# The last expert of a mixture layer worked in two halves, and ScalarE's read of a flag held behind seven experts' scatters

## The chip, the cores and the metric

The kernel runs on one core of a Trainium2 chip. The metric is the device time of one execution in microseconds (us), here the median of three runs. TensorE (PE) multiplies, VectorE (DVE) and ScalarE (ACT) do elementwise work, GpSimd (POOL) also issues the indirect DMAs, SyncE (SP) issues the plain ones.

## What is computed

Two layers of attention and feed-forward on x, 4 x 512 rows of 128 numbers. The change touches only the last piece, the second layer's mixture of experts with "expert choice": each of 8 experts takes the 256 rows that it scores highest, works them, and adds its result to those rows of the output.

```
route_prob = softmax(xf @ Ws + bs).T                 # [8, 2048]
route_vals, routes = top_k(route_prob, k)            # k = 256 rows for each expert
xin = xf[routes]
h = gelu(einsum('ekd,edf->ekf', xin, W1) + b1[:, None, :])      # 128 -> 512
out = (einsum('ekf,efd->ekd', h, W2) + b2[:, None, :]) * route_vals[..., None]
final = zeros.at[routes.reshape(-1)].add(out.reshape(-1, D))
```

## The kernel before

The program is written engine by engine; each engine runs its own list in order and waits on semaphores. About 150 us go to the two attentions, the first feed-forward layer and the search for each expert's rows. Then comes the stage of the change, `experts(again)`, written once for each engine, with `again` 0 here.

**Groups.** `GROUPS` lists pieces of work as (expert, first half, end half), where a half is 128 of an expert's 256 rows (`SH` is 2). Expert 0 is two groups of one half, experts 1 to 7 one group of two halves each, so `NG` is 9. Here k is a group's place in the list.

**One group.** GpSimd gathers each half's rows from DRAM (`gather`, L1936), which raises `got[e]`; expert 0's first half has a semaphore of its own, `got_first`. TensorE turns the rows (`rows_T`, L1337); ScalarE copies them out of PSUM (L858); TensorE makes the four chunks of the hidden layer (L1351); ScalarE puts bias and gelu on each (L863); TensorE makes y (L1363); VectorE adds a bias (L1736) and multiplies by the routing weight (L1738), which raises `y_done`. Then GpSimd adds each half's 128 rows to the output by an indirect DMA (`scatter`, L1944), which raises `out_add` by 16 when it has landed. Each of the 16 steps comes from one of the 16 DMA engines.

**What sets the order.** On GpSimd the list is: scatter both halves of expert e, gather the second half of e + 2, gather the first half of e + 3. So the first half of expert 7 is gathered ahead of expert 5's scatters, and its second half behind them. A scatter waits twice: for its group's `y_done`, and for the landing of all scatters of earlier experts, since two additions to one row must not cross:

```
pool.wait_ge(y_done, again * NG + (h + 1 if e == 0 else e + 2))
if n >= 1:
    pool.wait_ge(out_add, 16 * SH * n)
```

TensorE puts ten multiplications of no use (L911) between one group's y and the next group's turning, which keep its clock up. It turns group k + 1 right behind group k.

**The end.** Each engine, when through with its groups, reads a flag from memory and branches: if it is set, the whole work is done again by a slow general path, whose code stands between this point and the end of the engine's list; it isn't set here. ScalarE does so at L877 and L878, TensorE at L1375, VectorE at L1782. GpSimd reads the flag ahead of expert 6's scatters and branches at L1970 behind the last scatter. SyncE waits for all 16 scatters to land (`out_add` at 256). All engines then meet, which shows as line L102.

Of the kernel before, what the change touches and what calls it, by code (L numbers as in the profile page):

```python
# [33 lines left out]
E, F = 8, 512  # L34
FC = F // P
CAP = B * T // E
SH = CAP // P
# [6 lines left out]
BITS = 30  # L44
HEAD_GROUPS = ((0, 6), (6, 6), (12, 4))
FAST, SLOTS = 2, CH
GROUPS = ((0, 0, 1), (0, 1, 2)) + tuple((e, 0, SH) for e in range(1, E))
NG = len(GROUPS)
WARM = 10
INDEX_GROUPS = ((0, 1), (1, 4), (4, 8))  # L50
# [4 lines left out]

def chunk_rows(c):
    return min(CW, GK - c * CW)


def index_group(e):  # L60
    return [g for g, (e0, e1) in enumerate(INDEX_GROUPS) if e0 <= e < e1][0]
# [36 lines left out]
def program(nc, a, out):  # L98
# [3 lines left out]
    with ExitStack() as ctx:  # L102
# [3 lines left out]
        def sem(name):  # L106
            return ctx.enter_context(nc.semaphore(name))
# [131 lines left out]
        def logits(ps):  # L239
# [21 lines left out]
        ld_w = [sem(f"ld_w{e}") for e in range(E)]  # L261
        out_base, out_add = sem("out_base"), sem("out_add")
        rows_out = [sem(f"rows_out{b}") for b in range(B)]
        got_first, got = sem("got_first"), [sem(f"got{e}") for e in range(E)]
        consts_set, ctxT_ps_done, ctxT_done = sem("consts_set"), sem("ctxT_ps_done"), sem("ctxT_done")
        w_4_done = sem("w_4_done")
        k4_ps_done, k_hi_done, k_lo_done, k_stack_done, k_max_done = (
# [27 lines left out]
        xinT_ps_done, xinT_done, h_ps_done, gelu_done, y_ps_done, y_done = (  # L295
            sem(n) for n in ("xinT_ps_done", "xinT_done", "h_ps_done", "gelu_done", "y_ps_done", "y_done"))
# [53 lines left out]
        for n in range(E + 1):  # L350
# [5 lines left out]
            ("store", 32))  # L356
        LOADS = 32
        NAN_N, TILE_N = sum(n for _, n in NAN), sum(n for _, n in TILE)
        AFTER_NAN = LOADS + NT * NAN_N
        FLAGGED = 5  # L360
        TURNS_ALL = AFTER_NAN + FLAGGED + NT * TILE_N

        class Turns:


            def __init__(self, eng, stages, name, at):
                self.eng, self.at, self.k = eng, at + sum(n for _, n in stages[:[m for m, _ in stages].index(name)]), 0
# [113 lines left out]
        def run_tile(eng, i):  # L481
# [77 lines left out]
            if eng is nc.tensor:  # L559
# [7 lines left out]
                for g in range(G):  # L567
                    for c in range(GC):
                        n, o = chunk_rows(c), c * D + g * GD
                        go(); go.end(eng.matmul(bank[0][:, g * GD:(g + 1) * GD], wT[0:n, c, g, :], spans["v8"][0:n, o:o + GD],  # L570
                                                start=(c == 0), stop=(c == GC - 1)))
# [119 lines left out]
        def _(act):  # L691
# [72 lines left out]
            for ph in range(B):  # L764
                b = ph
                for s in range(SLOTS):
# [7 lines left out]
                    if b < B - 1:  # L774
                        n = chunk_rows(s // G)
                        nc.scalar.activation(pT[0:n, b % 2, s, :], ST_ps[s % 2][0:n, :], ACT.Exp).then_inc(exp_done, 1)  # L776
                    else:
                        half, i0 = 2 * s // SLOTS, s * PIECES % CH
                        n = chunk_rows(i0 // G)
                        nc.scalar.activation(pT[0:n, b % 2, i0:i0 + PIECES, half * HT:(half + 1) * HT],  # L780
                                             ST_ps[s % 2][0:n, :].rearrange("p (i t) -> p i t", i=PIECES), ACT.Exp).then_inc(exp_done, 1)
# [71 lines left out]
            def experts(again):  # L853

                for k, (e, h0, h1) in enumerate(GROUPS):
                    n, rows = again * NG + k, slice(h0 * P, h1 * P)
                    act.wait_ge(xinT_ps_done, n + 1)
                    nc.scalar.copy(xinT[:, k % 2, rows], bank[k % 2][:, rows]).then_inc(xinT_done, 1)  # L858
                    if n >= 2:
                        act.wait_ge(y_ps_done, n - 1)  # L860
                    for c in range(FC):
                        act.wait_ge(h_ps_done, n * FC + c + 1)
                        nc.scalar.activation(hg[:, k % 2, c, rows], bank[2 + c][:, rows], ACT.Gelu_apprx_tanh,  # L863
                                             bias=b1[:, e * FC + c:e * FC + c + 1]).then_inc(gelu_done, 1)

            def indices(again):

                act.wait_ge(own_base_done, again + 1)
                for e in range(E):
                    ins = nc.scalar.activation(cumx[:, e, :], pre[:], ACT.Identity, bias=own_base[:, e:e + 1], scale=own[:, e:e + 1])  # L870
                    if e + 1 in [e1 for _, e1 in INDEX_GROUPS]:
                        ins.then_inc(cumx_done, 1)

            act.wait_ge(once_done, 3)
            indices(0)
            experts(0)
            act.wait_ge(flag_done, 1)  # L877
            with act.If(act.value_load(flag[0:1, 0:1], min_val=0, max_val=1) > 0):  # L878
                with act.Fori(0, NT) as i:
# [7 lines left out]
        def _(pe):  # L887
# [438 lines left out]
            def rows_T(again, k):  # L1326
                n, (e, h0, h1) = again * NG + k, GROUPS[k]
                if h1 == 1:
                    pe.wait_ge(got_first, 16 * (again + 1))
                else:  # L1330
                    pe.wait_ge(got[e], 16 * (again + 1) * (h1 - h0))
                if k >= 2:
                    pe.wait_ge(xinT_done, n - 1)
                else:
                    pe.wait_ge(idx_done, again * len(INDEX_GROUPS) + k + 1)
                for h in range(h0, h1):
                    ins = pe.transpose(bank[k % 2][:, h * P:(h + 1) * P], xin[:, e, h, 0:D], ident)  # L1337
                ins.then_inc(xinT_ps_done, 1)

            def experts(again):  # L1340
                rows_T(again, 0)
                for k, (e, h0, h1) in enumerate(GROUPS):
                    n, rows = again * NG + k, slice(h0 * P, h1 * P)
# [52 lines left out]
        def _(dve):  # L1396
# [159 lines left out]
            with nc.allow_low_precision("a shift of the exponent that numerator and denominator share"):  # L1556
# [174 lines left out]
                def experts(again):  # L1731

                    for k, (e, h0, h1) in enumerate(GROUPS):
                        hs, shape = slice(h0, h1), [P, h1 - h0, D]
# [88 lines left out]
        def _(pool):  # L1823
# [71 lines left out]
            for ph in range(B):  # L1895
# [14 lines left out]
                if ph == 2:  # L1910
                    rows(0, 0)
            (ua, a0, a1, _, _), (ub, b0, b1_, _, _) = units(B - 1)
            t = B - 2
            ln_rstd(1, B - 1, ua, a0, a1)
# [14 lines left out]
            last_row = pool.to_reg(B * T - 1)  # L1929

            def gather(again, e, h):
                if (e, h) == (0, 0):
                    pool.wait_ge(idx_first, again + 1)
                else:
                    pool.wait_ge(idx_done, again * len(INDEX_GROUPS) + index_group(e) + 1)
                nc.gpsimd.indirect_dma_start(xin[:, e, h, :], None, gather_rows, bass.IndirectOffsetOnAxis(idx[:, h, e:e + 1], 0),  # L1936
                                             bounds_check=last_row, oob_is_err=False).then_inc(got_first if (e, h) == (0, 0) else got[e], 16)

            def scatter(again, e, h):
                n = again * E + e  # L1940
                pool.wait_ge(y_done, again * NG + (h + 1 if e == 0 else e + 2))
                if n >= 1:
                    pool.wait_ge(out_add, 16 * SH * n)
                nc.gpsimd.indirect_dma_start(flat, bass.IndirectOffsetOnAxis(idx[:, h, e:e + 1], 0), y[:, e, h, :], None,  # L1944
                                             bounds_check=last_row, oob_is_err=True, compute_op=ALU.add).then_inc(out_add, 16)

            def experts(again, first, last):

                for e in range(first, last):
                    if e == 0:  # L1950
                        for ahead in range(2):
                            for h in range(SH):
                                gather(again, ahead, h)
                        gather(again, 2, 0)
                    for h in range(SH):
                        scatter(again, e, h)
                    if e + 2 < E:
                        gather(again, e + 2, 1)
                    if e + 3 < E:
                        gather(again, e + 3, 0)  # L1960
# [38 lines left out]
```

## Time and profile before

| what | value |
|---|---|
| median of 3 runs | 217.88 us (217.6 to 218.38) |
| the profiled execution | 216.2 us, of which the span of the profile is 214.4 us |
| mean granted TensorE clock | 0.988 |
| busy in the span | PE 182.4, DVE 130.8, POOL 101.9, ACT 88.2 us |
| scatters (L1944) | 16, together 25.5 us of GpSimd |
| gathers (L1936) | 16, together 17.8 us of GpSimd |
| DMA queue q8, instructions | 12 packets, 0.20 MB |
| DMA queue q14, instructions | 12 packets, 0.10 MB |

The span runs from the first to the last instruction; 1.8 us of the profiled execution lie around it. A scatter's or gather's time on GpSimd is that of writing its descriptors; the data moves later, on queue q0. Queues q8 and q14 carry the program's own instructions to the engines, in one packet each time.

### The profile page before, as it was taken

To read this page: it belongs to the slowest core of one execution; us is meant where nothing else is said; L and a number is where in the kernel's file an instruction comes from. 1 tells how busy PE (TensorE), PEld (TensorE's weight loads), DVE (VectorE), ACT (ScalarE), POOL (GpSimd) and SP (SyncE) were. 2 spreads that over 40 slices of the span, in tenths; PEclk is the share of its full clock that TensorE was granted. 3 is DMA by queue.
4 is the path that set the end of the run, shared out by engine and by line. 5 is a ranking of instruction groups with operands and counts; after the bars stand their busy time and mean duration, and the time that the engine had idled before them with its cause. 6 is when DMAs were issued, how large, how long until landed. Compare 5 with 4: busy or idle time off the path is not lost.

```text
span 214.4 us, 3571 instructions
## 1 busy us (share of the span) xinstructions
PE 182.4 (85%) x1231; PEld 109.8 (51%) x1236; DVE 130.8 (61%) x450; ACT 88.2 (41%) x206; POOL 101.9 (48%) x111
## 2 busy tenths in 40 slices
PE   7988997979999978999999997998789877897730
PEld 2643543335334545376765764332277666786630
DVE  5887699077865889586789788887918111110110
ACT  2432772242622574246544452466443331333210
POOL 0699628000253022811048498200576788788722
PEclk9999999999999999999999999999999999999995
DMA  6634212111000001089810202100113232332313
GB/s 186 187 94 137 73 44 54 34 31 46 24 0 3 0 0 49 5 249 330 269 44 0 100 5 101 52 0 0 29 42 37 27 48 39 41 37 38 37 23 29
DMA packets 16127, 13.64 MB, mean 64 GB/s; under 512 B 3699, under 2 KB 13079, under 8 KB 16103
## 3 DMA queue, kind: packets, MB, share of 16 engines
q1 hardware_dynamic: 12246, 10.61, 16.6%
q0 software_dynamic: 2944, 2.30, 8.2%
q10 hardware_dynamic: 913, 0.43, 0.8%
q8 instruction: 12, 0.20, 0.4%
q14 instruction: 12, 0.10, 0.1%
HBM read 8.02 MB, written 3.21 MB: 52 GB/s over the span
## 4 chain that ended last, share of the span: by engine, by line
PE 41%; DVE 23%; POOL 14%; issue 10%; DMA 5%; ACT 3%; POOLq 1%; DVEq 0%
POOL out L1944 8%; PE psum L1009 7%; DVE mrow L1525 5%; DMA out<-pT,idx 4%; DVE pT L1671 3%; PE psum L906 3%; POOL pT L1936 3%; PE psum L1027 3%; DVE stats L1407 3%; PE psum L916 3%; DVE le L1721 2%; PE psum L979 2%; PE psum L1090 2%; PE psum L950 2%; PE psum L1046 2%
## 5 line engine op out<-in xcount | busy, mean ns | idle before, releaser
L1834 POOL TENSOR_SCALAR ve<-mv 128x4 f32<-128x4 f32 (+1 forms) x19 | 4.4, 232 | 69.4 <-DVE mv L1410 69.3
L776 ACT ACTIVATE pT<-psum 103x512 f32<-103x512 f32 (+1 forms) x36 | 21.2, 596 | 30.2 <-PE psum L981 30.2
L1944 POOL DMA_INDIRECT out<-pT,idx x16 | 25.5, 1594 | 11.2 <-issue 4.2
L1936 POOL DMA_INDIRECT pT<-gather_rows,idx x16 | 17.8, 1112 | 21.1 <-DVE idx L1725 17.1
L1525 DVE TENSOR_REDUCE mrow<-psum 128x8 bf16<-128x616 f32 x32 | 24.6, 788 | 5.1 <-PE psum L950 5.1
L906 PE MATMUL psum<-c 128*128 128x512 bf16 x103 | 26.5, 379 | 1.2 <-ACT key_map L801 1.0
L1736 DVE TENSOR_TENSOR pT<-psum,b_rows 128x256 f32<-128x256 f32 (+1 forms) x9 | 3.5, 394 | 36.2 <-PE psum L1363 36.2
L1351 PE MATMUL psum<-xinT,w 128*128 128x256 f32 (+1 forms) x72 | 16.2, 368 | 4.4 <-ACT xinT L858 3.2
L1552 DVE RECIPROCAL rden<-psum 128x512 f32<-128x512 f32 (+1 forms) x5 | 13.6, 2716 | 6.7 <-PE psum L1009 6.0
L1363 PE MATMUL psum<-w,pT 128*128 128x128 f32 x128 | 17.4, 284 | 0.2 <-DVE flag L1744 0.2
L863 ACT ACTIVATE pT<-psum,b 128x256 f32<-128x256 f32 (+1 forms) x36 | 14.4, 450 | 7.7 <-PE psum L1351 7.6
L1363 PEld LDWEIGHTS psum<-w,pT 128*128 128x128 f32 x128 | 16.2, 191 | 1.4 <-DVE flag L1744 0.3
L1351 PEld LDWEIGHTS psum<-xinT,w 128*128 128x128 f32 x72 | 12.0, 190 | 7.6 <-ACT xinT L858 5.9
L701 ACT COPY xnT<-psum 128x512 f32<-128x512 f32 (+1 forms) x19 | 9.8, 515 | 13.4 <-PE psum L916 13.3
L979 PE MATMUL psum<-q_stack,k_stack 128*103 128x512 f16 (+1 forms) x36 | 14.4, 401 | 0.8 <-DVE mT L1530 0.6
L906 PEld LDWEIGHTS psum<-c 128*128 128x128 bf16 x108 | 9.9, 99 | 9.6 <-ACT key_map L801 1.5
L858 ACT COPY xinT<-psum 128x256 f32<-128x256 f32 (+1 forms) x9 | 3.1, 349 | 26.7 <-PE psum L1337 26.7
L1838 POOL TENSOR_TENSOR rstd<-ve,half_neg 128x4 f32<-128x4 f32 (+1 forms) x14 | 13.4, 955 | 1.2
L981 PE MATMUL psum<-mT,neg_head 128*103 128x512 bf16 (+1 forms) x36 | 13.6, 379 | 0.0
L950 PE MATMUL psum<-k_max,q_hi 32*128 32x308 f16 x64 | 9.4, 299 | 4.3 <-DVE mrow L1525 3.9
L1846 POOL TENSOR_SCALAR xrow<-res,mv,rstd 128x128 f32<-128x128 f32 x16 | 12.6, 798 | 0.1
L950 PEld LDWEIGHTS psum<-k_max,q_hi 32*128 32x128 f16 x64 | 2.9, 91 | 16.2 <-DVE mrow L1525 10.7
(198 smaller groups left out, 370.3 us busy)
## 6 DMA issues: line engine op xcount, KB each, us to landing
w<-in_L_ffn_W SPq DMA_DIRECT2D x16, 256.0 KB, 5.5
gather_rows<-xrow SPq DMA_DIRECT2D x4, 272.0 KB, 2.1
x<-in_x SPq DMA_DIRECT2D x4, 256.0 KB, 4.1
q_stack<-q_hi SPq DMA_DIRECT2D x32, 32.0 KB, 1.8
out<-res SPq DMA_DIRECT2D x4, 256.0 KB, 2.1
q_stack<-q_lo SPq DMA_DIRECT2D x24, 32.0 KB, 1.9
b_rows<-in_L_ffn_b SPq DMA_DIRECT2D x1, 512.0 KB, 3.9
pT<-gather_rows,idx POOLq DMA_INDIRECT x16
```

The source lines that it names most:

```text
L776: nc.scalar.activation(pT[0:n, b % 2, s, :], ST_ps[s % 2][0:n, :], ACT.Exp).then_inc(exp_done, 1)
L863: nc.scalar.activation(hg[:, k % 2, c, rows], bank[2 + c][:, rows], ACT.Gelu_apprx_tanh, bias=b1[:, e * FC + c:e * FC + c + 1]).then_inc(g ...
L906: pe.matmul(bank[b][:, :], ident16, c16[:, 0:4 * P], start=True, stop=True)
L950: pe.matmul(bank[to + k][:, 0:GK], q_hi[rows, b % 2, j * P:(j + 1) * P], k_max[rows, b].rearrange("p h k -> p (h k)"), start=True, stop=Tr ...
L979: pe.matmul(ST_ps[s % 2][0:n, :], k_stack[:, b, g].rearrange("p h k -> p (h k)")[:, o:o + n], q_stack[:, b, g, :], start=True, stop=False)
L981: pe.matmul(ST_ps[s % 2][0:n, :], neg_head[:, g * GK + o:g * GK + o + n], mT[:, b % 2, :], start=False, stop=True).then_inc(st_ps_done, 1)
L1009: ins = pe.matmul(to[g * GD:(g + 1) * GD, :], lhsT, pT[0:n, b % 2, c * G + g, :], start=(c == 0), stop=(c == GC - 1), tile_position=(0, g ...
L1351: pe.matmul(bank[2 + c][:, rows], w1[:, e, c * P:(c + 1) * P], xinT[:, k % 2, rows], start=True, stop=True).then_inc(h_ps_done, 1)
L1363: ins = pe.matmul(bank[6 + k % 2][:, h * P:(h + 1) * P], hg[:, k % 2, c, h * P:(h + 1) * P], w2[:, e, c, :], start=(c == 0), stop=(c == FC ...
L1525: dve.tensor_reduce(mrow[:, b % 2, u // 2, h0:h0 + 2 * GH].rearrange("p (c h) -> p c h", c=2), psum[:, to:to + 2, 0:GK].rearrange("p c (h ...
L1936: nc.gpsimd.indirect_dma_start(xin[:, e, h, :], None, gather_rows, bass.IndirectOffsetOnAxis(idx[:, h, e:e + 1], 0), bounds_check=last_row ...
L1944: nc.gpsimd.indirect_dma_start(flat, bass.IndirectOffsetOnAxis(idx[:, h, e:e + 1], 0), y[:, e, h, :], None, bounds_check=last_row, oob_is_ ...
```

## The change

The last expert becomes two groups, (7, 0, 1) and (7, 1, 2), as expert 0 was already. Its first half gets a gather semaphore of its own. GpSimd's scatter of each half of expert 7 waits for that half's `y_done` alone. ScalarE, through with its groups, waits until `out_add` shows the landing of the scatters of experts 0 to 6, and reads the flag after that.

```diff
-GROUPS = ((0, 0, 1), (0, 1, 2)) + tuple((e, 0, SH) for e in range(1, E))
+GROUPS = ((0, 0, 1), (0, 1, 2)) + tuple((e, 0, SH) for e in range(1, E - 1)) + ((E - 1, 0, 1), (E - 1, 1, 2))
...
+def group_of(e, h):
+    return [k for k, (of, h0, h1) in enumerate(GROUPS) if of == e and h0 <= h < h1][0]
...
-        got_first, got = sem("got_first"), [sem(f"got{e}") for e in range(E)]
+        got_half, got = {e: sem(f"got_half{e}") for e in (0, E - 1)}, [sem(f"got{e}") for e in range(E)]
...
             experts(0)
+            act.wait_ge(out_add, 16 * SH * (E - 1))
             act.wait_ge(flag_done, 1)
...
-                    pe.wait_ge(got_first, 16 * (again + 1))
+                    pe.wait_ge(got_half[e], 16 * (again + 1))
...
-                                             bounds_check=last_row, oob_is_err=False).then_inc(got_first if (e, h) == (0, 0) else got[e], 16)
+                                             bounds_check=last_row, oob_is_err=False).then_inc(got_half[e] if e in got_half and h == 0 else got[e], 16)
...
-                pool.wait_ge(y_done, again * NG + (h + 1 if e == 0 else e + 2))
+                pool.wait_ge(y_done, again * NG + group_of(e, h) + 1)
```

In TensorE's list, behind the y of expert 6 and its ten idle multiplications, the last expert stands like this before (a row says line, operation, tiles, shape and count; `got7` is the landing of both halves' gathers):

```order
L1337 MATMUL psum<-c,pT 128x128 [waits xinT_done,got7]
L1337 MATMUL psum<-c,pT 128x128
L1351 MATMUL psum<-xinT,w 128x256 [waits gelu_done,ld_w7,xinT_done]
L1351 MATMUL psum<-xinT,w 128x256 [waits gelu_done] x3
L1363 MATMUL psum<-w,pT 128x128 [waits gelu_done,y_done]
L1363 MATMUL psum<-w,pT 128x128 [waits gelu_done] x3
L1363 MATMUL psum<-w,pT 128x128 x4
L1375 TENSOR_LOAD flag [waits flag_done]
```

And with the change (line numbers are 5 higher); behind these rows stand the same four rows of L1356 and L1368 once more, and then the read of the flag:

```order
L1342 MATMUL psum<-c,pT 128x128 [waits xinT_done,got_half7]
L1356 MATMUL psum<-xinT,w 128x128 [waits gelu_done,ld_w7,xinT_done]
L1356 MATMUL psum<-xinT,w 128x128 [waits gelu_done] x3
L1368 MATMUL psum<-w,pT 128x128 [waits gelu_done,y_done]
L1368 MATMUL psum<-w,pT 128x128 [waits gelu_done] x3
L916 MATMUL psum<-c 128x256 x10
L1342 MATMUL psum<-c,pT 128x128 [waits xinT_done,got7]
```

The first half no longer waits for the second half's gather, and ten more idle multiplications stand between the halves. In ScalarE's list the end was this:

```order
L858 COPY xinT<-psum 128x256 [waits xinT_ps_done]
L863 ACTIVATE pT<-psum,b 128x256 [waits h_ps_done,y_ps_done]
L863 ACTIVATE pT<-psum,b 128x256 [waits h_ps_done] x3
L878 TENSOR_LOAD flag [waits flag_done]
L878 ISA x2
L878 COMPARE_AND_BRANCH
```

and is this with the change, for the second half, which follows the same three rows for the first:

```order
L862 COPY xinT<-psum 128x128 [waits xinT_ps_done]
L867 ACTIVATE pT<-psum,b 128x128 [waits h_ps_done,y_ps_done]
L867 ACTIVATE pT<-psum,b 128x128 [waits h_ps_done] x3
L883 TENSOR_LOAD flag [waits flag_done,out_add]
L883 ISA x2
L883 COMPARE_AND_BRANCH
```

Five operations of 256 columns became ten of 128, and the read of the flag waits for `out_add` too. GpSimd's list is the same in both, but for what its last two scatters wait for.

## Rows read from the trace of the kernel before

**Rows 1.** The chain that ended last, its end: start us, us, what.

```profile
192.79 0.21 POOL pT L1936
...
196.26 3.23 DMA out<-pT,idx
...
201.84 0.30 issue
202.15 4.58 DMA out<-pT,idx
...
206.75 0.02 POOLq L1943
...
207.49 0.36 POOL out L1944
```

**Rows 2.** Timeline of the last expert: start, us, engine, line, operation, idle before.

```profile
198.77 1.25 PE L911 MATMUL psum<-c 128*128 128x256 bf16 x10
...
200.83 0.44 PE L1337 MATMUL psum<-c,pT 128*128 128x128 f32 x2 [0.81 <-DMA pT<-gather_rows,idx]
...
202.53 1.71 ACT L863 ACTIVATE pT<-psum,b 128x256 f32<-128x256 f32 x4 [0.85 <-PE psum L1351]
...
206.17 0.43 DVE L1738 TENSOR_TENSOR pT<-pT 128x256 f32<-128x256 f32 x1
...
209.35 1.56 POOL L1944 DMA_INDIRECT out<-pT,idx  x1 [0.30 <-issue]
```

**Rows 3.** DMA in the window 204.2 to 206.2 us: busy tenths in slices of 0.05 us, queues.

```profile
DMA  0998975999998622100000000002712220000000
...
q8 instruction: 1, 0.02, 2.8%
q14 instruction: 1, 0.01, 1.6%
```

**Rows 4.** DMA in the window 205.5 to 206.2 us: packets, MB, share of 16 engines.

```profile
q0 software_dynamic: 9, 0.00, 9.9%
```

**Rows 5.** Source lines L878 and L1375: the branches of ScalarE and TensorE, ns.

```profile
L878 ACTq COMPARE_BRANCH  x1: 54/54/54, 204.5 to 204.5; - x1
...
L1375 PEldq COMPARE_BRANCH  x1: 3761/3761/3761, 205.2 to 205.2; - x1
```

**Rows 6.** Source line L102, the meeting at the end: durations in ns, start us.

```profile
L102 POOLq DRAIN  x1: 5881/5881/5881, 208.3 to 208.3; - x1
...
L102 SPq COMPARE_BRANCH  x1: 38/38/38, 212.7 to 212.7; - x1
```

**Rows 7.** Timeline of expert 0's second half, and of a turning without a wait.

```profile
157.94 0.27 PE L1337 MATMUL psum<-c,pT 128*128 128x128 f32 x1
...
158.25 0.27 ACT L858 COPY xinT<-psum 128x128 f32<-128x128 f32 x1 [0.69 <-PE psum L1337]
...
158.57 1.16 PE L1351 MATMUL psum<-xinT,w 128*128 128x128 f32 x8 [0.36 <-issue]
...
159.14 1.36 ACT L863 ACTIVATE pT<-psum,b 128x128 f32<-128x128 f32 x4 [0.62 <-PE psum L1351]
...
159.57 1.47 PE L1363 MATMUL psum<-w,pT 128*128 128x128 f32 x8
...
161.40 0.29 DVE L1738 TENSOR_TENSOR pT<-pT 128x128 f32<-128x128 f32 x1
...
161.98 1.57 POOL L1944 DMA_INDIRECT out<-pT,idx  x1 [1.22 <-DVE pT L1738]
...
165.50 1.25 PE L911 MATMUL psum<-c 128*128 128x256 bf16 x10
...
166.59 0.44 PE L1337 MATMUL psum<-c,pT 128*128 128x128 f32 x2
```

**Rows 8.** DMA in the window 206.2 to 208.2 us.

```profile
q8 instruction: 1, 0.02, 4.1%
```

**Rows 9.** DMA in the window 209.5 to 211.3 us: GB/s in slices of 0.045 us, queues.

```profile
GB/s 0 0 46 46 410 23 57 57 80 159 159 137 148 91 103 91 46 34 23 23 0 0 0 0 0 0 0 0 182 0 0 0 0 0 0 0 0 0 0 11
...
q8 instruction: 1, 0.02, 5.5%
```

## The prediction, made before the changed kernel ran

> **What bounds the kernel now.** I read the page first for where the stage of the change lies, then the chain that ended last, since only its end is touched, then the timeline for the work behind each wait, and last the DMA windows, because the chain ends in a DMA.
>
> The chain runs through GpSimd. Its last link but one is a landing: the second scatter of expert 6 starts at 202.15 and is on the chain for 4.58 us, to 206.73; the wait on `out_add` passes at 206.75, and expert 7's first scatter starts at 207.49 [rows 1]. The values for it were ready at 206.17 + 0.43 = 206.60 [rows 2]. So two things end almost together there, the landing (206.73) and the values (206.60), and taking away one alone gives little. The second scatter follows when GpSimd is through with the first, 1.86 us later, at 209.35 [rows 2]. SyncE sees all landed at 212.7, and GpSimd's drain, begun at 208.3, lasts 5.88 us, to 214.2 [rows 6], just ahead of the span's end at 214.4. Landing and drain both hang on the last scatter: it starts at 209.35, and the rest of the span is 5.05 us.
>
> The reader should compare the two landings on the chain: 3.23 us from the start of expert 5's second scatter, 4.58 for expert 6's [rows 1]. The DMA window shows why. The scatter's packets run from 204.25 to 205.1; then almost nothing; then some work again from 205.5 [rows 3], and this is 9 packets of q0, the last of the scatter [rows 4]. In between, q8 moved one packet of instructions, 2.8% of 16 engines over 2 us = 0.90 us [rows 3]. One DMA engine was held by it, and this engine's 9 packets came late. A 16-fold semaphore is complete only with its slowest engine. The price is 4.58 - 3.23 = 1.35 us of landing.
>
> The Trainium skill (DMA: Bandwidth & Descriptors, "Queues, rings and completion order") says that a DMA engine turns from one queue to the next only between packets. The trace agrees: the 9 packets stood behind one packet of 0.90 us.
>
> **The change, part by part.** I date expert 7 anew.
>
> *First half, values.* Its gather was issued at 192.79 [rows 1], seven us ahead of need. Before, the turning stood at 200.83, held by the second half's gather [rows 2]. Now it follows the idle multiplications, as in expert 1's case, 166.59 - 165.50 = 1.09 us behind their start [rows 7]: 198.77 + 1.09 = 199.86. A half costs what expert 0's second half did [rows 7]: from turning to copy 0.31, from copy to hidden layer 0.32, from hidden layer to finished values 161.69 - 158.57 = 3.12. So values at 199.86 + 0.63 + 3.12 = 203.61, 3.0 us before 206.60. This is early enough; nothing waits for it.
>
> *Second half, values.* TensorE is through with the first half's y at 200.49 + (161.04 - 158.57) = 202.96 [rows 7]. The ten added idle multiplications stand behind it: turning at 202.96 + 1.09 = 204.05, values at 204.05 + 0.63 + 3.12 = 207.80. That is 1.2 us later than before, so the split delays the last values. The least bound is 0.2 lower, since part of expert 0's half ran beside the half ahead of it. The added ten cost 1.1 us of this; they are hidden only as long as GpSimd is busy with the first scatter.
>
> *The wait on ScalarE.* It stands behind the last gelu, 204.68 + 159.14 + 1.36 - 158.57 = 206.61; behind the waiting flag read there is no work on ScalarE, only the branch. Seven experts' scatters should have landed by then, so the wait costs nothing, and, for the same reason, adds little: the split alone moves ScalarE's branch from 204.5 [rows 5], which is 0.3 behind its last gelu's end at 204.24 [rows 2], to about 206.9.
>
> *The landing of expert 6.* With no packet of instructions in its way, it takes 3.23 as in the case before: 202.15 + 3.23 = 205.38. If one is still in the way, 4.58. I take 3.23: the branch that preceded the q8 packet goes away from here.
>
> *The scatters.* First: landing to start took 207.49 - 206.73 = 0.76 [rows 1], so 205.38 + 0.76 = 206.14 (values, 203.61, are long there). Second: by GpSimd 206.14 + 1.86 = 208.00; by its values 207.80 + 0.29 (161.98 - 161.69 [rows 7]) = 208.09. The later counts: 208.09 against 209.35, a gain of 1.26; by the lesser bound 1.35. I take 1.3.
>
> *The end.* From the last scatter's start on all stays: 209.35 - 1.3 = 208.05, plus 5.05 = 213.1 for the span, and 216.2 - 1.3 = 214.9 for the profiled execution. The median of the runs shown, 217.88, is 1.7 above that execution; I take the same 1.3 off it: **216.6 us**. One part alone would give less: the wait alone leaves values at 206.60, start 206.89, gain 0.6; the split alone the whole, if ScalarE's branch is the cause.
>
> **The rivals.**
>
> *The packet isn't ScalarE's.* The branch at 204.5 and the q8 packet soon after it stand together, but TensorE's stream may have asked for the packet by itself. For this: ScalarE's branch lasts only 54 ns and so waited for nothing, while TensorE's lasts 3761 ns [rows 5]; the packet that follows TensorE's branch is on q8 too [rows 8], and the one that follows ScalarE's by 1.1 us is on q14 [rows 3]. If so, the packet goes where the added instructions of TensorE's list put it, probably up to 2 us earlier, among expert 6's first scatter's packets; but if it meets the second scatter again, the first scatter of expert 7 stays at 207.49 and there is no gain: 217.9.
>
> The Trainium skill (Runtime: NRT & Kernel Launch, "Instruction fetch mechanics") has the sequencer fetch the next block of instructions by itself, and a taken branch wait for a fetch only where its target lies outside of what is loaded. The 3761 ns of TensorE's branch agree, and by this rule the rival above is the right reading of the q8 packet.
>
> *The last scatter is hit instead (the other side).* TensorE's branch stands 0.96 us behind the last gelu (204.24 to 205.2), so at 206.61 + 0.96 = 207.6. One q8 packet follows within 1.05 us of it and lasts 4.1% of 16 x 2 us = 1.3 [rows 8], so to about 209.9. Another began at 209.7, 4.5 us behind the branch, and lasted 5.5% of 16 x 1.8 = 1.6 us [rows 9]; now at 212.1. The last scatter's packets would run from 208.05 + 2.1 to 208.05 + 2.95 (204.25 and 205.1 less 202.15), so 210.15 to 211.0, between the two packets. The near side leaves 0.25 us. If a packet lands inside, the end is 1.35 later for one of 0.9 us, and up to 2.05 for one of 1.6: 217.9 to 218.6. It decides as soon as an instruction packet on the same DMA engine starts before 211.0 and ends after it. Against: it needs one engine in 16 to be the same, which the trace doesn't settle (it was the same for the one packet above), and the drain might not hang on the landing.
>
> *The second half's values come late.* Each 0.1 us beyond 207.8 is lost. With 0.5 more: 217.1. It would take 1.3 more to lose all.
>
> **How the numbers follow.** Forecast (216.1 to 217.1): 0.58. Packet not ScalarE's and again in the way, 217.9: 0.16. Last scatter hit, 217.9 to 218.6: 0.18, of which 0.10 slower. Values late, near 217.1: 0.08. A change under 0.3% (0.65 us) can't be told from none. Faster is 0.58 + 0.08, less 0.02 for a mix of cases = 0.64; same 0.16 + 0.08 + 0.02 = 0.26; slower 0.10. The range runs from 216.1 (forecast less 0.5 for scatter between runs) to 218.1, which leaves out 0.15 or so above and below.
>
> **What the profile would show.** First half turned at 199.9, values at 203.6; second half's values near 207.8 or a little less; wait on `out_add` passed at 205.4; last two scatters at 206.1 and 208.0 to 208.1; span 213.1. If the first stands at 207.5 still, the packet was not ScalarE's or another took its place; if both start early and the span is no shorter, the last landing was hit. I am wrong if instruction packets, which no engine in this program controls, fall into the shifted windows.

## The result, and the profile after

The changed kernel took 216.3 us in the median of 20 runs, the kernel before 217.69 (20 runs). The ratio is 0.9937, with a 95% interval of 0.9909 to 0.9965: faster, by 1.4 us. The ratio leaves out executions over 1.5% above the fastest of their kernel; the two medians don't. Forecast were 216.6 and a gain of 1.3. A second comparison of the same two kernels (experiment 5) gave 0.9999 (0.9953 to 1.0044) and shows no gain, so the size rests more on the profiles than on the measured times: single executions of either kernel spread from 214.7 to 224 us. The profiled execution took 215.9 us, its span 213.7.

The chain of the changed kernel, at the place of [rows 1] (start us, us, what):

```profile
202.78 3.27 DMA out<-pT,idx
...
206.07 0.02 POOLq L1948
...
206.81 1.12 POOL out L1949
```

Expert 6's second landing takes 3.27 us, not 4.58. This execution reached its second scatter 0.63 us later than that of before, for reasons upstream; so I measure from there. Let the **tail** be the time from the start of expert 6's second scatter to the end of the span. It was 214.4 - 202.15 = 12.25 us, and is 213.7 - 202.78 = 10.92.

The timeline of the last expert, in place of [rows 2]:

```profile
200.45 0.27 PE L1342 MATMUL psum<-c,pT 128*128 128x128 f32 x1
...
201.08 1.16 PE L1356 MATMUL psum<-xinT,w 128*128 128x128 f32 x8 [0.36 <-ACT xinT L862]
...
203.72 0.29 DVE L1743 TENSOR_TENSOR pT<-pT 128x128 f32<-128x128 f32 x1
...
204.28 0.27 PE L1342 MATMUL psum<-c,pT 128*128 128x128 f32 x1
...
204.91 1.16 PE L1356 MATMUL psum<-xinT,w 128*128 128x128 f32 x8 [0.35 <-ACT xinT L862]
...
207.54 0.29 DVE L1743 TENSOR_TENSOR pT<-pT 128x128 f32<-128x128 f32 x1
...
208.67 1.56 POOL L1949 DMA_INDIRECT out<-pT,idx  x1 [0.30 <-issue]
```

The first half is ready at 204.01, the second at 207.83; the last scatter starts at GpSimd's own pace, 0.84 behind its values.

The branches of ScalarE and TensorE in the changed kernel, by source line (ns, start us), in place of [rows 5]:

```profile
L883 ACTq COMPARE_BRANCH  x1: 54/54/54, 206.9 to 206.9; - x1
L1380 PEldq COMPARE_BRANCH  x1: 3742/3742/3742, 207.6 to 207.6; - x1
```

And DMA in the changed kernel from 202.8 to 204.8 us (slices of 0.05 us), in place of [rows 3]:

```profile
GB/s 0 0 0 0 338 51 61 20 51 51 82 133 123 143 154 133 113 62 31 10 0 0 0 0 0 0 0 10 10 10 20 10 0 10 10 0 0 0 0 0
...
q8 instruction: 1, 0.02, 3.6%
```

A packet counts where it starts, so the 338 GB/s is the 16 KB packet, at 203.0. It is still there; it now stands 0.3 us behind the second scatter's start, not 2.5. It lasts 3.6% of 16 x 2 us = 1.15 us, to 204.2. The last packets of the scatter ahead follow from 204.15 on, so it is that scatter which is held up; its packets are over by 204.8, and the chain waits for the other, to 206.05. The next window, 204.8 to 206.1 us, holds expert 6's second scatter and nothing else, unbroken:

```profile
DMA  0009499466699999999976201100000000000000
...
q0 software_dynamic: 144, 0.07, 53.7%
```

The meeting at the end, in place of [rows 6]:

```profile
L106 POOLq DRAIN  x1: 5110/5110/5110, 208.4 to 208.4; - x1
...
L106 SPq COMPARE_BRANCH  x1: 38/38/38, 212.0 to 212.0; - x1
```

SyncE sees all landed at 212.0 and the drain ends at 213.5, 1.5 later, as before (212.7 and 214.2).

ScalarE's branch is at 206.9, 3.9 us behind the packet, so it didn't bring the packet. Counted in the traces, TensorE had begun 2525 of its recorded instructions when the packet started in the kernel before, and 2524 in the changed one: the packet kept its place in TensorE's list, and TensorE got there sooner.

### The profile page after: what moved, and what is told of

It is laid out like the page before. It is cut to its first block, busy times and chain, and to the rows that moved or that the text cites. A ratio compares the mean times of both kernels' runs of the same rounds, so it can differ in the third digit from the quotient of the medians.

```text
span 213.7 us, 3624 instructions
## 1 busy us (share of the span) xinstructions
PE 184.4 (86%) x1254; PEld 111.5 (52%) x1254; DVE 131.6 (62%) x452; ACT 88.9 (42%) x211; POOL 101.9 (48%) x111
## 4 chain that ended last, share of the span: by engine, by line
PE 41%; DVE 21%; POOL 15%; issue 10%; DMA 6%; ACT 3%; POOLq 1%; DVEq 0%
POOL out L1949 8%; PE psum L1014 7%; DVE mrow L1530 5%; POOL pT L1941 4%; DMA out<-pT,idx 3%; PE psum L911 3%; DVE pT L1676 3%; PE psum L1032 3%; DVE stats L1412 3%; PE psum L921 3%; PE psum L984 2%; PE psum L1095 2%; PE psum L955 2%; PE psum L1051 2%; PE psum L1083 2%
## 5 line engine op out<-in xcount | busy, mean ns | idle before, releaser
L911 PE MATMUL psum<-c 128*128 128x512 bf16 x108 | 27.6, 379 | 1.0 <-ACT key_map L805 1.0
L1356 PE MATMUL psum<-xinT,w 128*128 128x256 f32 (+1 forms) x80 | 16.6, 350 | 4.8 <-ACT xinT L862 4.4
L1368 PE MATMUL psum<-w,pT 128*128 128x128 f32 x128 | 17.4, 284 | 0.2 <-DVE flag L1749 0.2
L1368 PEld LDWEIGHTS psum<-w,pT 128*128 128x128 f32 x128 | 16.1, 190 | 1.2 <-DVE flag L1749 0.3
L1356 PEld LDWEIGHTS psum<-xinT,w 128*128 128x128 f32 x80 | 12.5, 190 | 8.0 <-ACT xinT L862 6.5
```

Of the source, the lines that this page charges most:

```text
L911: pe.matmul(bank[b][:, :], ident16, c16[:, 0:4 * P], start=True, stop=True)
L1356: pe.matmul(bank[2 + c][:, rows], w1[:, e, c * P:(c + 1) * P], xinT[:, k % 2, rows], start=True, stop=True).then_inc(h_ps_done, 1)
L1368: ins = pe.matmul(bank[6 + k % 2][:, h * P:(h + 1) * P], hg[:, k % 2, c, h * P:(h + 1) * P], w2[:, e, c, :], start=(c == 0), stop=(c == FC ...
```

## The experiments

**Theory T**: the packet that held up the landing belongs to TensorE's own stream of instructions; the split moved it out of the way, and let the first scatter start before the second half's values are ready; ScalarE's wait does nothing. **Rivals**: the packet is ScalarE's, and its wait or its later branch removes it (S, W); the packet hangs on a place in the program (P); the earlier values alone bring the gain (V).

All numbers but the ratios are from one profile of each; the tail is the yardstick. Experiments 8 to 12 are single executions, so they give no ratio; 9 to 12 ran on another chip than 1 to 8, where one execution of the kernel before took 215.66 us. "First" is the start of expert 7's first scatter, counted from the start of expert 6's second.

| kernel | second scatter of expert 6 | its landing | first | tail | ratio to before |
|---|---|---|---|---|---|
| before | 202.15 | 4.58 | 5.34 | 12.25 | 1 |
| changed | 202.78 | 3.27 | 4.03 | 10.92 | 0.9937 (0.9909 to 0.9965) |
| 1 split alone | 201.36 | 3.24 | 4.00 | 10.94 | 1.0007 (0.9954 to 1.0061) |
| 2 wait alone | 202.05 | 4.19 | 4.95 | 11.85 | 1.0013 (0.9974 to 1.0052) |
| 3 before, 24 instructions fewer | 202.16 | 4.07 | 4.82 | 11.74 | 1.003 (0.9981 to 1.008) |
| 4 changed, 22 fewer | 204.14 | 3.28 | 4.05 | 11.16 | 1.0015 (0.9976 to 1.0054) |
| 5 changed, again | 201.63 | 3.35 | 4.11 | 11.17 | 0.9999 (0.9953 to 1.0044) |
| 6 before, 60 fewer | 201.44 | 3.38 | 4.66 | 11.76 | 1.0004 (0.996 to 1.0047) |
| 7 changed, waits in other order | 203.72 | 3.29 | 3.56 | 10.58 | 0.9944 (0.9905 to 0.9982) |
| 8 changed, branch later | 203.42 | 3.31 | 4.07 | 11.08 | one execution, 216.62 us |
| 9 changed, halves later | 203.35 | 3.30 | 4.06 | 11.05 | one execution, 216.55 us |
| 10 changed, both values | 203.81 | 3.31 | 5.47 | 13.29 | one execution, 219.28 us |
| 11 changed, no gap | 203.21 | 3.56 | 4.32 | 12.29 | one execution, 217.74 us |
| 12 changed, branch latest | 201.80 | 3.4, not on the chain | 4.17 | 12.70 | one execution, 216.67 us |

The second column spreads by 2.8 us where the list ahead is all but the same, more than twice the effect, and I take this to be what blurs the ratios. One cause can be read. TensorE's mean granted clock (third from the end of the numbers) and busy times from 33 to 41 us in experiment 9:

```profile
33.00:41.00 8.00, 6.88 (x44) 2.50 (x44) 4.86 (x9) 1.15 (x2) 4.33 (x3) 0.79 0.20 49
```

and in the kernel before:

```profile
33.00:41.00 8.00, 7.05 (x58) 3.03 (x60) 4.49 (x8) 1.85 (x6) 3.96 (x3) 1.00 0.19 48
```

In experiment 9 the clock was at 1.2 GHz for some 3 of these 8 us. Its first gather started at 153.9 us, against 151.9 in the kernel before and 152.8 in the changed one. The profiles of experiments 7, 8, 10 and 11 show a dip to 7 tenths in the same stretch. It isn't the whole cause: the changed kernel had no dip there and yet stood 0.9 us behind the kernel before.

**1. The split alone.**

```diff
             experts(0)
-            act.wait_ge(out_add, 16 * SH * (E - 1))
             act.wait_ge(flag_done, 1)
```

> The changed kernel without ScalarE's wait for the seven experts' scatters. Theory T (the packet of instructions that held up expert 6's landing belongs to TensorE's own stream; ScalarE's wait does nothing): the same time as the changed kernel, about 0.994 of the kernel before; the q8 packet stands near the start of expert 6's first scatter's packets, expert 6's second landing takes 3.2 to 3.4 us on the chain. Rival S (ScalarE's branch causes the packet): since ScalarE's branch moves behind its added gelus anyway, also nearly the same. Rival W (the wait is what brings the gain): 4.5 us of landing and a ratio of 1.000.

Its chain:

```profile
201.36 3.24 DMA out<-pT,idx
...
205.36 1.19 POOL out L1948
```

The tail is 10.94 against 10.92: the wait does nothing. The ratio, 1.0007, would say that the split does nothing either; its interval begins at 0.9954, overlaps that of the changed kernel, and is nearly twice as wide as the effect.

**2. The wait alone.** The kernel before, with that one line added.

> The kernel before with ScalarE's wait alone. Theory T: the 16 KB packet on q8 still stands at 204.6 us and expert 6's second landing still takes over 3.9 us, less than 4.58 at most by what the 8 KB packet on q14 behind ScalarE's branch added; gain 0 to 0.5 us, ratio 0.998 to 1.000. Rival S: the q8 packet goes, the landing takes 3.3 us, the values (0.29 behind 206.60) bind instead: gain 0.6 us, ratio 0.997.

Its chain, the DMA from 204.1 to 206.1 us, and ScalarE's branch:

```profile
202.05 4.19 DMA out<-pT,idx
```

```profile
GB/s 0 369 51 31 31 51 82 82 102 123 133 133 123 92 62 41 31 20 10 10 10 10 10 10 10 10 0 0 0 0 0 0 0 0 0 0 328 0 0 0
```

```profile
L879 ACTq COMPARE_BRANCH  x1: 54/54/54, 207.0 to 207.0; - x1
```

ScalarE branches at 207.0 and the packet came at 204.2 nevertheless. This settles that ScalarE's branch doesn't bring it. The tail is 0.4 shorter than before, as the packet stood 2.1 and not 2.5 us behind the scatter's start; why it came sooner isn't known. The 328 GB/s at 205.9 is the packet behind TensorE's branch.

**3. Fewer instructions ahead, in the kernel before.**

```diff
-                            warm_rows(WARM, (k + 1) % 2)
+                            warm_rows(WARM - 2, (k + 1) % 2)
```

> The kernel before with 8 in place of 10 idle multiplications ahead of each of experts 2 to 7, 24 instructions fewer in TensorE's list, so that TensorE branches away before its stream reaches the place at which the q8 packet was asked for. ScalarE is as before. Theory T: no q8 packet of 16 KB between 203 and 205.5 us, landing of expert 6's second scatter 3.2 to 4.0 us in place of 4.58, first scatter of expert 7 held by its values at 206.9 or by the landing at 207.0: gain 0.4 to 0.6 us, ratio near 0.9975. Rival S: the packet and the 4.58 us stay, ratio 1.000.

DMA from 203.9 to 205.9 us:

```profile
GB/s 328 0 0 0 0 0 0 20 51 51 41 61 92 113 123 164 143 92 82 52 41 41 21 41 21 20 10 10 10 10 0 0 0 164 0 0 0 0 0 0
...
q8 instruction: 1, 0.02, 3.5%
```

A miss: the packet is there, 1.8 us behind the scatter's start, earlier than in the kernel before and not gone. That it stays is what Rival S said; experiment 2 rules S out all the same. The landing, 4.07, is shorter than before only because the packet ended earlier. In the kernel before and in experiments 2 and 3 the landing ends 1.2 us behind the packet's end: 205.5, 205.1 and 205.1 (start, and length by the share of a window) against 206.73, 206.24 and 206.23.

**4. Fewer instructions ahead, in the changed kernel.**

```diff
-                            warm_rows(WARM, (k + 1) % 2)
+                            warm_rows(WARM - (2 if k < 7 else 1 if k == 7 else 0), (k + 1) % 2)
```

> The changed kernel with 11 idle multiplications fewer ahead of experts 2 to 7 (22 instructions fewer in TensorE's list). ScalarE as in the changed kernel, wait included. Theory T: the q8 packet comes some 2 us later than in the changed kernel, near 205 us, into the packets of expert 6's second scatter; the landing takes 4 to 4.6 us in place of 3.27 and the gain of the change shrinks by 0.7 to 1.3 us: ratio 0.997 to 1.000. Rival S: landing 3.3 us, ratio 0.994 as the changed kernel.

A miss: landing 3.28, tail 11.16. The packet stood at 204.06, 0.1 ahead of the scatter's start, and not behind it. A landing of 3.3 is what Rival S expected here; it is experiment 2 that rules S out. What moved was the clock; busy times and clock of the windows 174 to 181 and 188 to 195 us:

```profile
174.00:181.00 7.00, 6.24 (x31) 5.42 (x32) 0.32 (x1) 2.27 (x5) 5.32 (x5) 0.76 0.29 39
```

```profile
188.00:195.00 7.00, 6.03 (x28) 4.97 (x29) 0.00 (x0) 2.26 (x5) 5.43 (x5) 0.76 0.30 39
```

With two idle multiplications fewer TensorE's clock fell to 1.2 GHz twice for some 3 us, and expert 6's scatter came at 204.14. Experiment 3, also with two fewer ahead of each, kept its clock at 1.00 in both windows, so this is a risk and not a rule.

**5. The changed kernel again.**

> The changed kernel once more, unaltered, since single executions here spread by over 1%, and its measured ratio of 0.994 should be told apart from the 1.001 of the split alone. Theory T (the split brings the whole gain): ratio 0.992 to 0.998, and from the start of expert 6's second scatter to the end of the span 10.8 to 11.1 us, as with the split alone (10.9), against 12.26 before.

The tail held within 0.25 us (11.17), a little above the 10.8 to 11.1 expected. The ratio did not repeat: expected were 0.992 to 0.998, measured 0.9999. Weighing the two by the inverse squares of their intervals gives 0.9954, give or take 0.0024, that is 1.0 us; the tails say 1.1 to 1.3.

**6. The packet taken out of the kernel before.** The same idle columns in half as many instructions.

```diff
-                for _ in range(n):
-                    pe.matmul(bank[b][:, CAP:2 * CAP], ident16, c16[:, 0:2 * P], start=True, stop=True)
+                for _ in range(n // 2):
+                    pe.matmul(bank[b][:, :], ident16, c16[:, 0:4 * P], start=True, stop=True)
```

> The kernel before with 5 idle multiplications of 512 columns in place of each 10 of 256 ahead of experts 2 to 7: the same columns with 60 instructions fewer in TensorE's list, so that TensorE branches before its stream would reach the place at which the q8 packet was asked for. Theory T (packet of TensorE's own stream, tied to the number of instructions): no q8 packet between 202 and 205.5 us, expert 6's second landing 3.2 to 3.4 us, and the first scatter of expert 7 held by its values: from the start of expert 6's second scatter to the span's end 11.6 to 11.8 us against 12.26; ratio near 0.997. Rival P (the packet is tied to the place in the program or to ScalarE): packet at 204 to 205 us, landing 4.0 to 4.6.

Its chain:

```profile
201.44 3.38 DMA out<-pT,idx
...
204.84 0.02 POOLq L1943
204.86 1.00 issue
...
206.10 0.34 POOL out L1944
```

The values, in its timeline:

```profile
205.40 0.42 DVE L1738 TENSOR_TENSOR pT<-pT 128x256 f32<-128x256 f32 x1
206.10 1.56 POOL L1944 DMA_INDIRECT out<-pT,idx  x1 [3.10 <-DVE pT L1738]
```

DMA from 201.4 to 205.2 us has no q8 packet at all:

```profile
q0 software_dynamic: 288, 0.13, 38.8%
q14 instruction: 1, 0.01, 0.8%
```

As Theory T had it. Only TensorE's list was altered, so the packet goes with TensorE's list. The wait on landings passes at 204.84, and now the values are the gate: they are ready at 205.82, and the scatter starts 0.28 behind them. The tail is 11.76. So the packet costs 12.25 - 11.76 = 0.5 us in the kernel before, and no more, because the values bind next.

**7. The waits in the other order.** A candidate for a better kernel.

```diff
+                if (e, h) == (E - 1, 0):
+                    pool.wait_ge(out_add, 16 * SH * n)
                 pool.wait_ge(y_done, again * NG + group_of(e, h) + 1)
-                if n >= 1:
+                if n >= 1 and (e, h) != (E - 1, 0):
                     pool.wait_ge(out_add, 16 * SH * n)
```

> The changed kernel with the two waits of expert 7's first scatter in the other order: its values first, the landing second, so that the landing is what the DMA instruction itself waits for and the 0.5 us in which GpSimd's sequencer passes it on lie ahead of the landing. If the 0.76 us between landing and start is mostly this: start 0.27 to 0.3 behind the landing, the last scatter at GpSimd's pace 1.86 later, or 0.3 behind its values; from expert 6's second scatter to the end 10.4 to 10.5 us in place of 10.9. If the time is spent in the engine anyway: no change, 10.9.

```profile
203.72 3.29 DMA out<-pT,idx
...
207.28 1.56 POOL out L1951
...
209.14 1.56 POOL out L1951
```

Landing to start is 0.27 us in place of 0.76. In the traces the wait written second shows as a semaphore instruction of its own on GpSimd (L1943 in the kernel before), and the one written first doesn't: I take it that the DMA instruction carries it. With the landing written second, 0.51 us of issue lie between its passing and the instruction; with it written first they are gone. The tail, 10.58, is the shortest of all, if a little over the 10.4 to 10.5 expected. The ratio, 0.9944 (0.9905 to 0.9982), can't be told from the changed kernel's.

**8 and 12. TensorE's branch later.** 22, then 36 idle multiplications behind its last y.

```diff
             experts(0)
+            warm_rows(22, 0)
             pe.wait_ge(flag_done, 1)
```

> The changed kernel with 22 more idle multiplications behind TensorE's last y, so that its branch, and the q8 packet about 1.0 us behind it, come some 2 us later, at 210 to 211 us, among the last scatter's packets. If the end hangs on the landing of the last scatter: landing 1.2 us behind the end of the packet, 0.4 to 1.3 later than without, and the span's end later by the same (from expert 6's second scatter to the end 11.3 to 12.2 us). If GpSimd's drain runs for a set time from its last instruction: SyncE's branch is late, the span's end isn't (10.9).

A miss: the packet ended at 211.5, as the last scatter's packets began; nothing was held, and the tail is 11.08, not 11.3 to 12.2. It tells nothing of the drain. So once more, with 36:

> As the changed kernel with TensorE's branch late, with 36 idle multiplications in place of 22, since the packet with 22 ended just as the last scatter's packets began. The q8 packet then starts 2.3 to 2.8 us behind the last scatter's start. If the end hangs on the landing: landing 1.2 us behind the packet's end, 4.6 to 5.2 us in place of 3.3, and the tail from expert 6's second scatter 12.2 to 12.9 us. If GpSimd's drain runs for a set time: tail 10.9 to 11.1.

Experiment 12's last scatter, and DMA from 209.8 to 212.8 us (slices of 0.075 us):

```profile
207.83 1.56 POOL L1950 DMA_INDIRECT out<-pT,idx  x1 [0.30 <-issue]
```

```profile
DMA  0099986799862000000003000121200000000000
GB/s 0 0 48 48 280 61 75 96 116 116 96 69 27 7 0 0 0 0 0 0 0 109 0 0 7 14 14 7 14 0 0 0 0 0 0 0 0 0 0 0
...
q8 instruction: 1, 0.02, 3.2%
```

```profile
L106 POOLq DRAIN  x1: 6705/6705/6705, 207.5 to 207.5; - x1
...
L106 SPq COMPARE_BRANCH  x1: 38/38/38, 212.7 to 212.7; - x1
```

This is the rival of the other side, made on purpose. A packet of 3.2% x 16 x 3 = 1.54 us begins at 210.1 among the scatter's packets; the scatter's last ones come from 211.6 on. SyncE sees the landing 4.9 us behind the start, not 3.3, and the drain ends at 214.2, again 1.5 behind. The tail is 1.8 us longer than that of the changed kernel. The end hangs on the landing.

**9. Both halves later.** Meant to put the packet back in the way of the changed kernel.

```diff
-                            warm_rows(WARM, (k + 1) % 2)
+                            if k < 7:
+                                warm_rows(WARM, (k + 1) % 2)
+                            elif k == 7:
+                                warm(12, 0)
```

> The changed kernel with 12 idle multiplications of 512 columns in place of 10 of 256 ahead of the last expert's first half (1.75 us more), and none between its halves. TensorE's stream reaches the q8 packet's place 1.75 us later, the values of both halves stay ahead of GpSimd (first near 205.8, second near 208.5 in the changed kernel's time). Theory T (the gain comes from the packet leaving the landing's way): q8 packet 1.8 to 2.2 us behind the start of expert 6's second scatter, landing 1.18 us behind the packet's end, so 4.0 to 4.4 us, and the tail from that scatter's start to the span's end 11.7 to 12.1 us. Rival V (the gain comes from the earlier values alone): tail 10.9 to 11.1.

Inconclusive: there was no q8 packet from 201.5 to 209.1 us, so nothing could be in the way, and the theories say the same. The values came at 206.23 and 208.96 (timeline), 1.65 and 0.56 us later against expert 6's scatter than in the changed kernel, and cost nothing (tail 11.05):

```profile
207.41 1.56 POOL L1952 DMA_INDIRECT out<-pT,idx  x1 [2.50 <-DMA out<-pT,idx]
...
209.28 1.56 POOL L1952 DMA_INDIRECT out<-pT,idx  x1 [0.31 <-DVE pT L1746]
```

**10. The first half's scatter waits for both values.**

```diff
-                pool.wait_ge(y_done, again * NG + group_of(e, h) + 1)
+                pool.wait_ge(y_done, again * NG + group_of(e, h if e < E - 1 else SH - 1) + 1)
```

> The changed kernel, but the scatter of the last expert's first half waits for the values of both halves. Theory T: values of the second half stand 5.05 us behind the start of expert 6's second scatter in the changed kernel (207.83 against 202.78), so the scatter starts 0.3 later, at 5.3 to 5.4 in place of 4.0; tail 12.2 to 12.3 us, as before the change. If the packet's going were the whole gain: tail 11.7, as in the kernel before without the packet.

```profile
209.28 1.56 POOL L1949 DMA_INDIRECT out<-pT,idx  x1 [3.91 <-DVE pT L1743]
211.15 1.56 POOL L1949 DMA_INDIRECT out<-pT,idx  x1 [0.31 <-issue]
```

```profile
L106 SPq COMPARE_BRANCH  x1: 38/38/38, 215.4 to 215.4; - x1
```

The scatter starts at 5.47, 1.4 later than in the changed kernel and 0.1 later than before the change: the finer wait is what carries the early values through. The tail, 13.29, is 1 us more than I expected. SyncE saw the last landing at 215.4, 4.2 behind the scatter. A q8 packet of 1.3 us had begun at 212.95, 0.3 us ahead of the scatter's first packets, and ended at 214.25, among them.

**11. No idle multiplications between the halves.** As many are added ahead of experts 2 to 6.

```diff
-                            warm_rows(WARM, (k + 1) % 2)
+                            warm_rows(0 if k == 8 else WARM + (2 if k < 7 else 0), (k + 1) % 2)
```

> The changed kernel without the ten idle multiplications between the last expert's halves (two more ahead of each of experts 2 to 6 in their place). If they are hidden behind GpSimd's first scatter, as the prediction's sum has it (8.00 against 8.09): the second half's values 1.1 us earlier, the last scatter still 1.86 us behind the one ahead, tail 10.9 to 11.1. If the last scatter waits for its values: the tail shorter by up to 1 us.

Its chain, its last scatter, DMA from 211.2 to 213.2 us, and the two engines' ends:

```profile
203.21 3.56 DMA out<-pT,idx
```

```profile
209.39 1.56 POOL L1949 DMA_INDIRECT out<-pT,idx  x1 [0.30 <-issue]
```

```profile
GB/s 0 328 0 0 0 0 51 51 31 61 72 61 92 123 143 154 123 113 92 41 185 0 0 0 0 0 0 0 10 10 10 10 10 10 10 10 0 0 0 0
```

```profile
L106 SPq COMPARE_BRANCH  x1: 38/38/38, 213.8 to 213.8; - x1
```

```profile
L1380 PEldq COMPARE_BRANCH  x1: 3601/3601/3601, 206.9 to 206.9; - x1
```

The scatters stand 1.86 apart as before: the ten are hidden, as the sum had it. But the tail is 12.29. TensorE branched at 206.9, 3.7 behind expert 6's second scatter and not 4.8, so its second packet began at 211.3 and hit the last scatter, whose landing SyncE saw 4.4 us behind its start. Work that looked idle set when a packet came.

The stream's own packet moved too. It ran from 204.43 to 205.59, 1.2 us behind the start of expert 6's second scatter, and the landing, 3.56, ended again 1.2 us behind it. The first scatter moved by the same 0.29 us, to 4.32, though its values (204.50) were long there. So early values alone don't bring the gain (rival V); the landing must come early too. In experiment 12 the landing passed at 205.21, 1.2 us behind a packet that ended at 204.03.

## Why the prediction was right, point by point

**The landing.** Forecast 3.23, measured 3.27. That a packet of instructions among a scatter's packets holds up its landing is shown by experiments 6 and 12: without the packet 3.38, with one on purpose 1.6 more. That it does so by holding one DMA engine is the reading of [rows 3] and [rows 4]; the traces don't name the engine of a packet.

**Whose packet.** Here the forecast's step was wrong: "the branch that preceded the q8 packet goes away from here". It went with TensorE's list. The rival "the packet isn't ScalarE's" gave the right cause, and its first case is what happened: TensorE reached the place of the packet sooner, and the packet fell among the packets of the scatter ahead, 0.3 us and not 2.5 behind the start of the second. The turning no longer waits for the second half's gather (it stands 2.33 us ahead of expert 6's second scatter, not 1.32), and the first half has half the columns. So the forecast's landing, and with it the time, came right for a wrong reason: that the split moved the packet out of the way, and not only to another place in it, was luck as far as the forecast goes. I let two events 0.1 us apart outweigh the queue number and the 54 ns that spoke against it.

**The wait on ScalarE.** "Costs nothing" and "adds little" held: 10.94 without it. "The wait alone gains 0.6", with the landing at 3.23, didn't: the landing stayed at 4.19, and the 0.4 that the tail was shorter came with the packet's place.

**The values.** A half took 204.01 - 201.08 = 2.93 us from the hidden layer's start, not 3.12; expert 0's second half had run beside the first. From expert 6's second scatter the last values stood at 5.05 and not at 5.65, so the second scatter went by GpSimd (1.86) alone. That 207.83 meets the forecast 207.80 is chance: this execution ran 0.63 us later at that point.

**The scatters and the end.** First and second scatter at 3.99 and 5.94 forecast (5.90 with the gain of 1.3 that was taken), 4.03 and 5.89 measured; tail 10.95 forecast, 10.92 measured. The drain hangs on the landing (experiment 12), as was assumed.

**What each part gives.** The tail's 1.3 us are two gates gone together. The packet's going is worth 0.5 (experiment 6), and then the values bind; the split's early values, with a wait for each half, are worth the other 0.8 (11.76 to 10.94). Waiting for both halves' values gives none of it (experiment 10).

**The rival of the other side** didn't come in the changed kernel, but came in three neighbours of it (10 and 11 unasked, 12 on purpose), for 0.9 to 1.6 us of landing. Its 0.18 was not too much. The q8 packet behind the branch in the changed kernel ended at 209.9, by its share of the window and its start at 208.5, and the last scatter's packets began at 210.8. The next one began at 212.0, just behind the landing. Nothing in the kernel secures these distances.

**What stays open.** What makes TensorE's stream ask for its next packet just then. It goes with TensorE's list, but neither the number of instructions ahead (experiments 3 and 4) nor the place in the list (6 and 9) foretells it, and with the same list up to there it came 0.3 us behind the second scatter's start in the changed kernel and 1.3 behind it in experiment 12. A packet fully in the way of expert 6's landing was never seen in the changed kernel or its neighbours; the nearest, experiment 11, cost 0.3 us. And of two comparisons of the times only one shows the gain.

## What to carry to other kernels

When a short chain of indirect DMAs ends a kernel, look at what else moves on the DMA engines there: one packet of instructions among a scatter's packets made its landing 0.8 to 1.6 us late. If two gates stand within 0.2 us of each other, take both or neither; and where a GpSimd DMA has two waits, write the one that ends later first (0.27 us from landing to start in place of 0.76). Compare such a change by the stretch that it touches: the whole spread here by more than twice the gain.

## What the runs showed of the hardware that I had not expected

The end of this kernel, which branches over unused code, is a place of traffic. TensorE's branch lasted 3.4 to 4.2 us in the 14 traces, ScalarE's 54 ns. Two 16 KB packets on q8 followed TensorE's branch, 1.0 to 1.8 and 4.2 to 5.2 us behind its start, of 0.9 to 1.6 us each. The Trainium skill (Runtime: NRT & Kernel Launch, "Instruction fetch mechanics") says that a taken branch waits for a fetch where its target isn't loaded; the length of TensorE's branch and the packets behind it agree. The runs add what such a packet does to a landing that is under way: 0.8 to 1.6 us more, with the landing 1.1 to 1.2 us behind the packet's end. GpSimd's drain ended 1.5 us behind the last landing that SyncE saw in all 14 traces.
